# Scores of a turn as one block behind the second T tile, instead of four slices between T tiles

## What is computed

```
# layer 0: masked attention, 8 heads of 32
scores = einsum('bhsd,bhtd->bhst', q, k) * SCALE
scores = where(mask, scores, -1e9)       # 6 fixed masks, 2 heads masked by adj | eye
out    = softmax(scores) @ v ; out @ Wo.T + bo
# layer 1: gated graph layer, 4 heads
Wh    = h @ W.T + bW
A_mat = tanh(where(adj, (Wh @ attn) @ Wh^T, 0))
ha    = relu(A_mat @ Wh) over the heads @ A_w.T
hf    = h @ fc_w.T
out   = hf * coeff + ha * (1 - coeff),  coeff = sigmoid(hf @ g1.T + ha @ g2.T + gbias)
```

## Time and profile before

| | |
|---|---|
| median of 3 runs | 1156.95 us (1155.82 to 1157.34) |
| profiled execution, whole | 1157.57 us |
| its span, first to last instruction | 1155.8 us |
| PE busy | 1123.6 us, 97% |
| DVE busy | 697.1 us, 60% |
| ACT busy | 511.6 us, 44% |
| POOL busy | 255.2 us, 22% |
| scores on PE, L448 | 2048 instructions, 43.7 us busy |

### The profile page before, as it was taken

The page is one execution under the profiler, slowest core; times in us unless marked ns, Lnnn a source line. Parts: engine busy times, 40 slices in busy tenths (PEclk is TensorE's granted clock), DMA queues, the critical chain, the costliest instruction groups (busy, mean ns, idle before and its releaser), DMA issues.

```text
span 1155.8 us, 24597 instructions
## 1 busy us (share of the span) xinstructions
PE 1123.6 (97%) x9756; PEld 912.6 (79%) x9756; DVE 697.1 (60%) x1321; ACT 511.6 (44%) x908; POOL 255.2 (22%) x232
## 2 busy tenths in 40 slices
PE   6899999999999999999999999999999999999996
PEld 5778888787887878888787888878788787887774
DVE  6655665757556675665757566575765667566543
ACT  4444363534536253453625436353453625445241
POOL 1622131222212222131122213122221222211100
PEclk9999999999999999999999999999999999999998
DMA  7001000010000001000010100001000100100000
GB/s 248 16 7 41 19 22 20 18 40 18 25 29 24 19 18 40 18 20 19 18 40 18 40 18 20 19 18 40 18 21 24 33 19 18 40 19 3 1 19 18
DMA packets 26699, 32.58 MB, mean 28 GB/s; under 512 B 4400, under 2 KB 23344, under 8 KB 26288
## 3 DMA queue, kind: packets, MB, share of 16 engines
q1 hardware_dynamic: 26672, 32.19, 8.5%
HBM read 23.80 MB, written 8.39 MB: 28 GB/s over the span
## 4 chain that ended last, share of the span: by engine, by line
PE 94%; DVE 2%; POOL 2%; ACT 1%; issue 0%; DMA 0%; POOLq 0%; DVEq 0%; SPq 0%
PE bankB L344 20%; PE bankB L345 19%; PE bankB L346 19%; PE bankA L344 6%; PE bankB L550 5%; PE bankA L345 5%; PE bankA L346 5%; PE bankB L534 5%; PE bankA L448 3%; PE bankA L461 3%; PE bankA L475 2%; PE bankB L598 1%; PE bankA L501 1%; POOL aw_hi L1121 0%; DVE hf L1043 0%
## 5 line engine op out<-in xcount | busy, mean ns | idle before, releaser
L750 ACT ACTIVATE T<-bankB 128x512 f32<-128x512 f32 x128 | 76.5, 598 | 131.0 <-PE bankB L346 131.0
L777 ACT ACTIVATE cat_hi<-bankB 128x512 fp32r<-128x512 f32 x128 | 76.6, 598 | 129.3 <-PE bankB L346 129.3
L868 DVE SCALAR_TENSOR_TENSOR cat_lo<-bankB,cat_hi 128x512 fp32r<-128x512 f32 x128 | 86.4, 685 | 51.2 <-ACT cat_hi L777 50.2
L1148 POOL TENSOR_TENSOR probs<-probs,den 128x512 f32<-128x512 f32 x64 | 72.5, 1143 | 173.9 <-DVE den L957 173.9
L344 PE MATMUL bankB<-hT_lo,g_hi 128*128 128x512 f32 x256 | 108.3, 423 | 0.2 <-ACT res L796 0.2
L344 PE MATMUL bankB<-U_lo,wt_hi 128*128 128x512 f32 x256 | 101.4, 396 | 1.8 <-DVE U_lo L868 0.3
L345 PE MATMUL bankB<-hT_hi,g_lo 128*128 128x512 f32 x256 | 100.6, 393 | 0.0
L345 PE MATMUL bankB<-U_hi,wt_lo 128*128 128x512 f32 x256 | 100.1, 391 | 0.0
L346 PE MATMUL bankB<-U_hi,wt_hi 128*128 128x512 f32 x256 | 99.8, 390 | 0.0
L345 PE MATMUL bankB<-cat_hi,aw_lo 128*128 128x512 f32 x256 | 99.7, 390 | 0.0
L346 PE MATMUL bankB<-hT_hi,g_hi 128*128 128x512 f32 x256 | 99.7, 390 | 0.0
(11 more groups left out here) (143 smaller groups left out, 2640.3 us busy)
## 6 DMA issues: line engine op xcount, KB each, us to landing
y<-in_x SPq DMA_DIRECT2D x16, 512.0 KB, 3.5
out<-res SPq DMA_DIRECT2D x16, 512.0 KB, 3.0
x_raw<-in_xT SPq DMA_DIRECT2D x15, 512.0 KB, 3.3
W_nat<-in_Wn SPq DMA_DIRECT2D x1, 1028.0 KB, 6.4
attn_nat<-in_attn SPq DMA_DIRECT2D x1, 1024.0 KB, 8.7
adjS_u<-in_adjS SPq DMA_DIRECT2D x32, 32.0 KB, 2.8
raw_A<-in_AwT SPq DMA_DIRECT2D x1, 1024.0 KB, 8.5
x_second<-in_xT SPq DMA_DIRECT2D x1, 512.0 KB, 10.6
```

The source lines that it names most:

```text
L750: take(act.activation(T[:, n % DC, n // DC, :], bank[:], ACT.Copy), "B", f"T{n}")
L777: act.activation(cat_hi[:, n, :], bank[:], ACT.Relu).then_inc(cat_hi_ready, 1)
L868: return dve.scalar_tensor_tensor(out=out, in0=bank, scalar=bias, in1=hi.bitcast(F32), op0=op, op1=ALU.subtract)
L1148: pool.tensor_tensor(view, view, den[:, j, :].unsqueeze(2).to_broadcast([P, NG, S]), ALU.mult) \
```

## The change

`turn` of TensorE places the scores of A. Before, a quarter of them follows each of T1, T2, T3 and T4: `SCORES_FROM = 1`; the first two quarters are banks 0 and 1 (graphs 0 to 3, then 4 to 7), the last two are banks 2 and 3. After, all of them follow T1: banks 0 and 1 for all graphs, and at once banks 2 and 3. The same matmuls run in the same order among themselves. No other engine's program is changed, and no DMA.

```
-SCORES_FROM = 1
...
                 for n in range(KC):
                     T_tile(B, n)
                     if A is None and n == 1:
                         res_T(B - 1)
-                    if A is not None and 0 <= n - SCORES_FROM < 4:
-                        two, part = (n - SCORES_FROM) // 2 * 2, (n - SCORES_FROM) % 2 * (NG // 2)
-                        scores(A, range(two, two + 2), range(part, part + NG // 2))
+                    if A is not None and n == 1:
+                        for two in (0, 2):
+                            scores(A, range(two, two + 2), range(NG))
```

## The result

The changed kernel takes 1148.1 us (median of 4 runs, 1147.9 to 1148.4), the kernel before 1156.9 us. The ratio is 0.9926, with a 95% interval from 0.9908 to 0.9943: 0.7% faster, as forecast (1148.1). The profiled execution went from 1157.57 to 1148.35 us, its span from 1155.8 to 1146.6. Measured once more in another session it took 1148.4 us, ratio 0.9935 (0.9918 to 0.9951). Two of the executions of the kernel before, in a later session, ran at a mean granted clock of 0.75 and 0.85 and took 1401 and 1254 us; they are left out of every comparison.

A forecast was written before the change was run, and what follows sets the result against it. PE, 97% busy, bounds the kernel; 13 loop turns gain 6.2 us and two others 2.6, together 8.9, taking 1157.57 to 1148.7, with the median 0.6 lower: 1148.1 us. Range 1143.5 to 1153.

The forecast's parts named there:

- What bounds the kernel: PE, busy 97% of the span, sets the time; shortening its stream helps unless another engine becomes late at the gathering.
- The 0.15 us of slack: In a loop turn the mask could come 0.15 us later relative to PE before PE's gathering waits: 0.29 less 0.14.
- What the block costs PE: Scores as one block take about 2.00 us to the next T tile, saving PE 1.16 us a turn (1.11 to 1.21).
- the lower bound: Least time for the scores block up to the next T matmul: 1.80 + 0.15 = 1.95 us.
- the start-up row: Start-up turn's row of the same 128 score instructions as one block: 2.05 us to the next product, taken as the most.
- What DVE gets of it: DVE's softmax stretch, started by the first exponential behind T4, moves only 0.31 us earlier in a turn (0.26 to 0.36).
- The mask against POOL: POOL's third scaling holds the waiting mask, which then precedes the fourth: 0.88 us from reciprocal's end to mask's end.
- The row of the start-up turn: DVE subtraction waiting behind POOL's third scaling got in before the fourth, lasting 0.96 us instead of 0.69.
- the other order: Rival: POOL's fourth scaling goes ahead of the waiting mask, gathering 0.53 us later in 13 turns; 1163.2 us, chance 0.11.
- The sum: Gathering 0.48 us earlier in each of 13 loop turns, 1.32 in turn(1, 0) and turn(15, 14): 8.9 us together.
- T4's move: T4, its copy and the first exponential come 0.31 us earlier in a loop turn (0.26 to 0.36).

The follow-up runs named there:

- the two cut blocks: Changed kernel, scores split into two halves: first behind T1, second behind T2, 1155.1 us; first behind T1, second behind T4, 1143.4 us.
- the moved exponential: Changed kernel with ACT's first exponential behind T3 instead of T4: 1142.3 us, ratio 0.9876.
- the early exponential with slices: Kernel before (four slices of scores) with ACT's first exponential behind T3 instead of T4: 1162.1 us, ratio 1.0050.

## Why the prediction was right

- *What bounds the kernel*: right in kind. The wait L549 for L973 came 15 times and in loop turns lasted 0.7 us, as written. The 0.15 us of slack was too much: it takes the step from the mask's end to the gathering, 0.14 us, from turn(15, 14), where in a loop turn that step is 0.24 us. So the slack was 0.29 - 0.24 = 0.05 us.
- *What the block costs PE*: 1.16 us a turn foreseen, 1.2 measured (T7 begins at 11.81 us of its turn, 13.00 before). The block took 475.91 - 473.96 = 1.95 us, the lower bound; what made it 2.05 in the start-up row is not shown.
- *What DVE gets of it*: 0.31 us foreseen; the reciprocal ends at 488.94 - 471.05 = 17.89 of the turn against 18.24 before, 0.35. That this, and not the 1.2, sets the gain is shown by the two cut blocks and by the moved exponential.
- *The mask against POOL*: 0.88 us from the reciprocal's end to the mask's end foreseen, 0.88 measured. The row of the start-up turn carried the sign. That POOL's third scaling holds the mask is shown by the kernel where it comes later (0.69 us), that the other order costs what was said by the early exponential with slices (+0.5 us a turn).
- *The sum*: 13 loop turns gained 0.41 us each instead of 0.48, 5.4 us for 6.2. The mis-sized term is the step from mask to gathering: 0.14 us, read from turn(15, 14), holds in that turn (1035.21 + 0.96 to 1036.32 in the changed kernel, 0.15), but in the loop it is 490.06 - 489.82 = 0.24. The 0.04 more of T4's move made up for part. turn(15, 14) gained 1.34 us and turn(1, 0), from its first score to that of the next turn, 1.32; 1.32 was foreseen for each.
- A part of the hit is luck. The forecast added up 8.9 us from these 15 turns, and they gave 5.4 + 1.3 + 1.3 = 8.0. What closed the distance lies outside them: in the profiled executions turn(1, 0)'s first score came at 64.40 us instead of 65.72, 1.3 us earlier, though the start-up turn is the same program, and the end lost 0.1. That makes 9.2 us, the difference of the spans. Of the 1.3 us only 0.1 was there when PE began the keys' product (57.23 against 57.33); the other 1.2 come in a stretch at the lower granted clock (1.2 GHz, a 128x512 matmul starts every 0.43 us), which ended earlier in the changed kernel. In the rows below the column third from the right is the granted clock as a share of full, first before, then after. When the changed kernel was profiled again, turn(1, 0)'s first score came at 65.08 us and the span was 1146.5 us all the same, because the end was shorter. Such shares vary between executions and are no part of the change.

```profile
60.00:65.00 5.00, 5.00 (x17) 3.93 (x16) 0.00 (x0) 1.92 (x3) 2.23 (x1) 0.68 0.02 3
60.00:65.00 5.00, 5.00 (x59) 3.94 (x61) 0.00 (x0) 2.47 (x4) 2.14 (x1) 0.95 0.00 0
```

The changed kernel's DVE rows of turn(15, 14), with PE's gathering:

```profile
1035.21 0.96 DVE L973 TENSOR_TENSOR Abuf<-Abuf,adjT_u 128x512 f32<-128x512 f32 x1
...
1036.32 0.92 PE L549 MATMUL bankB<-Abuf,h 64*128 64x256 f32 x6 [0.57 <-DVE Abuf L973]
```

## What to carry to other kernels

Where one engine is busy for 97% of the span, a saving in its stream is worth no more than the slack of the others at its next meeting point, and what the same change moves them forward; here 1.2 us a turn became 0.05 of slack and 0.36 by which the mask's end moved, 0.41. Measure both before the saving, and look for the cheapest lever on the engine that is then late (here one exponential, one reduction moved behind the mask, one scaling held): that brought the rest, 0.80 us a turn, and without the saving the same edits are worth 1.4 us in all. If DVE and GpSimd both read two operands from SBUF near the meeting point, work out who asks first to a few hundredths of a microsecond: an engine that gets ready earlier can make the kernel slower.

## What was not expected of the hardware

- The same wait costs more in the hardware loop: from the mask's end to the first gathering matmul 0.24 us in all 13 loop turns of the changed kernel, 0.15 us in turn(1, 0) and turn(15, 14), which are written out. The code differs there in that semaphores are compared with a value that depends on the loop's counter; that this is the cause was not tried.
- With the block behind T0, PE paused in the first pass after 119 of 128 small matmuls, for 0.74 and 1.65 us, without a releaser. Behind the longer pause the granted clock was 0.51 of full (the lower of its two levels, 1.2 GHz) over the 3 us from 68 to 71 us; behind the shorter it was 1.00 over the same 3 us.
- The 128 small matmuls cost PE 2.2 us a turn as one block (1.95 us to the next T matmul, the rest in the T tiles beside it) in place of 4 x 0.85 = 3.4 us in slices. Of the 3.4 us, 4 x 0.47 = 1.9 are the small matmuls' own steps and 4 x 0.38 = 1.5 come with the changes between 128-row and 32-row matmuls.
